# Layer 1 cluster attention of a four-layer decoder as one phase with unpadded heads, row tiles of 32, and key distances laid out with tokens on partitions

## The reference

```
def _affinity(t, centers, inv_two_sig2, amplitudes):
    t2 = jnp.sum(t * t, axis=-1, keepdims=True)
    c2 = jnp.sum(centers * centers, axis=-1)[None, :, None, :]
    tc = jnp.einsum('bhnd,hkd->bhnk', t, centers)
    d2 = jnp.maximum(t2 + c2 - 2.0 * tc, 0.0)
    return amplitudes[None, :, None, :] * jnp.exp(-d2 * inv_two_sig2[None, :, None, :])
q = split_heads(x @ W_q)
kk = split_heads(x @ W_k)
v = split_heads(x @ W_v)
...
q_aff = _affinity(q, centers, inv_two_sig2, amplitudes)
k_aff = _affinity(kk, centers, inv_two_sig2, amplitudes)
v_agg = jnp.einsum('bhnk,bhnd->bhkd', k_aff, v)
k_sum = jnp.sum(k_aff, axis=2)
num = jnp.einsum('bhnk,bhkd->bhnd', q_aff, v_agg)
den = jnp.einsum('bhnk,bhk->bhn', q_aff, k_sum) + EPS
out = num / den[..., None]
out = out.transpose(0, 2, 1, 3).reshape(b, n, dm)
return out @ W_o
```

## Time and profile before

| | us |
|---|---|
| median of 3 runs (4250.77 to 4256.24) | 4255.73 |
| the profiled execution | 4252.81 |
| its span, first to last instruction | 4251.0 |
| first DMA of the block to the start of its `centers` phase | 10.4 |
| `centers` | 6.0 |
| first normalisation, queries, keys and values | 26.9 |
| groups 0, 1, 2 | 93.6, 93.7, 93.7 |
| group 3 | 73.9 |
| the whole block | 398.2 |

### The profile page before, as it was taken

One profiled execution on the slowest core, in us unless ns is written; L12 is line 12 of the kernel. 1 busy time (PEld: TensorE's weight loads), 2 busy tenths in 40 slices (PEclk: granted clock), 3 DMA queues, 4 the chain that ended last, 5 costly groups with the idle time before them and its releaser, 6 DMA issues. The chain is left out here.

```text
span 4251.0 us, 54674 instructions
## 1 busy us (share of the span) xinstructions
PE 3446.1 (81%) x18236; PEld 2010.2 (47%) x18256; DVE 2230.5 (52%) x4573; ACT 1795.2 (42%) x4162; POOL 956.3 (22%) x1147
## 2 busy tenths in 40 slices
PE   6868559998588889963489989746799999998868
PEld 3535348876355545552245564534333333323535
DVE  5655534555333325537565535533688888864521
ACT  5847413332122214422255534301377777774311
POOL 2524434424200002210034442111111111111200
PEclk9978659999788879976689989858799999999979
DMA  9000326655100010000100000112200000000000
GB/s 308 22 17 1 131 91 208 210 170 152 60 0 0 0 41 1 1 30 0 47 1 1 1 1 21 51 67 70 82 16 16 16 16 23 16 1 22 1 22 20
DMA packets 153750, 207.56 MB, mean 49 GB/s; under 512 B 21699, under 2 KB 134212, under 8 KB 151652
## 3 DMA queue, kind: packets, MB, share of 16 engines
q1 hardware_dynamic: 139668, 166.50, 12.4%
q0 software_dynamic: 13824, 37.77, 2.7%
HBM read 115.98 MB, written 88.21 MB: 48 GB/s over the span
## 5 line engine op out<-in xcount | busy, mean ns | idle before, releaser
L3523 DVE TENSOR_REDUCE peaks<-ps 128x1 f32<-128x1024 f32 x512 | 608.6, 1220 | 147.9 <-PE ps L3469 142.7
L3551 ACT ACTIVATE attn<-ps 128x512 f32<-128x512 f32 x1024 | 535.4, 602 | 118.0 <-PE ps L3460 116.3
L3469 PE MATMUL ps<-keys,queries 96*128 96x512 bf16 x1024 | 396.3, 392 | 18.2 <-DMA keys<-parts 14.3
L3460 PE MATMUL ps<-queries,keys 99*128 99x512 bf16 x1024 | 389.9, 384 | 3.5 <-ACT attn L3551 2.7
L3482 PE MATMUL ps<-attn,head_values 128*32 128x512 f32 x2048 | 272.3, 604 | 0.0
L1040 POOL TENSOR_TENSOR attn_w<-attn_w,attn_share 128x512 f32<-128x512 f32 x128 | 133.0, 1044 | 514.9 <-DVE attn_share L928 514.9
L3460 PEld LDWEIGHTS ps<-queries,keys 99*128 99x128 bf16 x1024 | 99.0, 97 | 306.3 <-ACT attn L3551 222.0
L1729 PE MATMUL ps<-experts,tileT 128*128 x884 | 230.4, 383 | 4.3 <-issue 4.3
L1913 DVE COPY normed<-ps 128x256 f32<-128x256 f32 x221 | 93.7, 424 | 207.7 <-PE ps L1745 98.2
L1745 PE MATMUL ps<-experts,hiddenT 128*128 (+1 forms) x474 | 147.6, 394 | 28.1 <-DVE hiddenT L1922 25.1
L973 ACT ACTIVATE attn_w<-attn_w 128x512 f32<-128x512 f32 x128 | 80.2, 627 | 210.7 <-DVE attn_w L922 210.7
(11 more groups left out here) (600 smaller groups left out, 7390.0 us busy)
## 6 DMA issues: line engine op xcount, KB each, us to landing
tile_in<-routed_rows SPq DMA_DIRECT2D x244, 128.0 KB
expert_rows<-normed SPq DMA_DIRECT2D x221, 128.0 KB
routed_rows<-zeros SPq DMA_DIRECT2D x2, 8064.0 KB, 45.3
experts<-in_L_ffn_experts SPq DMA_DIRECT2D x4, 3072.0 KB
routed_rows<-zeros SPq DMA_DIRECT2D x1, 12160.0 KB, 62.6
experts<-in_L_ffn_experts SPq DMA_DIRECT2D x8, 1024.0 KB
parts<-parts SPq DMA_DIRECT2D x48, 128.0 KB, 1.8
queries<-parts SPq DMA_DIRECT2D x96, 64.0 KB, 2.2
```

The costliest lines, as they stand in the source:

```text
L3460: nc.tensor.matmul(bank(("score", n)), keys[h % 3][0:DEEP, sl(kt)], queries[h % 3][0:DEEP, sl(c, CHUNK)], start=True, stop=True).then_inc( ...
L3469: last = nc.tensor.matmul(k.ps[:, SB + p % PB, :], queries[h % 3][0:ROWS, sl(t)], keys[h % 3][0:ROWS, sl(c, CHUNK)], start=True, stop=True)
L3523: v.tensor_reduce(peaks[:, r % 2, i // 2, i % 2:i % 2 + 1], k.ps[:, at:at + 2, :], AX.XY, ALU.max).then_inc(s["maxed"], 1)
L3551: nc.scalar.activation(attn[:, n % RING, :], bank(("score", n)), ACT.Exp, scale=1.0 / 16.0).then_inc(s["read"], 1)
```

## The change

The phases from the first normalisation to the last addition become one phase, `affinity`, whose engines walk through slots g = -2 to 4. Heads are no longer padded: queries, keys and their squares are two tiles (T = 2) of 128 rows, eight heads each, and 32 rows hold a pair of heads. A **round** is one side, one tile, four pairs (R = 4): TensorE multiplies 32 rows at a time (`rows = sl(r, PAD)`), pair r into bank r of PSUM. For queries the table is stationary, as before. For keys the tokens are stationary and the table moves, so their affinities come out with tokens on partitions and the transposes go. Their scale is then no longer one number for a partition: it is multiplied into the tables beforehand, and the centers' squares times scale are added by a bf16 product of ones with three bf16 parts of them (`shift_parts`), four of 512 columns in a round. ScalarE takes the exponential straight from PSUM; the clip is a minimum with 1 afterwards, by VectorE in place. GpSimd makes all squares. The other work comes as **jobs** in the banks 4 to 7. The mix has the pooled values as the stationary operand (32 columns each), and the denominator is made in the same way from `sums`, so that the result is already turned; the division is over 512 tokens a tile.

```diff
+        def slot_work(g):
+            here, there = 0 <= g < GROUPS, 0 <= g + 1 < GROUPS
...
+            for i, kind in enumerate(("k", "k", "q", "q")):
+                if here:
+                    work.append(("round", kind, g, i % 2))
+                if i == 2 and 0 <= g - 1:
+                    work += [("project", g - 1, j) for j in range(GROUP)]
+                if there:
+                    work += [[("q", g + 1, 0)], [("q", g + 1, 1)], [("k", g + 1, 0)], [("k", g + 1, 1)]][i]
+            if here:
+                work += [("pool", g, j) for j in range(GROUP)]
+            if there:
+                work += [("v", g + 1, j) for j in range(GROUP)]
+            if 0 <= g + 2 < GROUPS:
+                work += [("x", g + 2, kt) for kt in range(KD)]
+            if here:
+                work += [(kind, g, t) for t in range(T) for kind in ("sum", "mix")]
+            return work
...
+                    if at:
+                        round_done(pe, "exped", ROUNDS[at - 1])
...
+                    if kind == "k":
+                        for r in range(R):
+                            every = shift_parts[:, R * t + r, :].unsqueeze(1).broadcast_to([P, GROUP, P])
+                            nc.tensor.matmul(k.ps[:, r, :], ones[:, :], every, start=True, stop=False)
+                    for part in range(2):
...
+                        if kind == "q":
+                            for r in range(R):
+                                rows = sl(r, PAD)
+                                last = nc.tensor.matmul(k.ps[:, r, :], table[rows, t, :], source[rows, t, :], start=part == 0, stop=part == 1)
+                        else:
+                            for j in range(GROUP):
+                                for r in range(R):
+                                    rows = sl(r, PAD)
+                                    last = nc.tensor.matmul(k.ps[:, r, sl(j)], source[rows, t, sl(j)], table[rows, t, :], start=False,
+                                                            stop=part == 1 and j == GROUP - 1)
...
-                        nc.vector.tensor_scalar(near[side][:, p, :], k.ps[:, m % 8, :], center2[:, p:p + 1], 0.0,
-                                                ALU.add, ALU.max).then_inc(s["bounded"], 1)
...
+                        v.tensor_scalar(tile, tile, 1.0, None, ALU.min).then_inc(s["capped"], 2)
...
+                    elif kind == "sum":
+                        last = v.tensor_scalar(share[:, i, :], source, 1e-6, None, ALU.add)
+                    else:
+                        link(v.reciprocal(share[:, i, :], share[:, i, :]))
+                        last = v.tensor_tensor(oT[:, i, :], source, share[:, i, :], ALU.mult)
...
+                for tile in (scales[:, :], key_scales[:, :, :]):
+                    link(v.tensor_scalar(tile, tile, 1e-3, None, ALU.max))
+                    link(v.tensor_tensor(tile, tile, tile, ALU.mult))
+                    link(v.reciprocal(tile, tile))
+                    link(v.tensor_scalar(tile, tile, -0.5, None, ALU.mult))
```

More of the change, by code:

```diff
@@ L2359, in l1_attn @@
     H, D, C = 16, 16, 64
-    PAIRS, T = H // 2, H * PAD // P
-    VW = D + 1
+    PAIRS, T, R = H // 2, 2, 4
+    VW, PW = D + 1, 2 * D
     n = "L1_attn_"
     with ExitStack() as stack:
-        wq, a = weights(k, stack, n + "W_q", KD, H * PAD)
-        wk, b = weights(k, stack, n + "W_k", KD, H * PAD)
+        wq, a = weights(k, stack, n + "W_q", KD, DIM)
+        wk, b = weights(k, stack, n + "W_k", KD, DIM)
         wv, c = weights(k, stack, n + "W_v", KD, DIM)
         wo, d = weights(k, stack, n + "W_o", KD, DIM)
[L2368 to L2383, removed]
@@ new lines, in l1_attn @@
+        centers, where = sb(k, stack, "centers", [P, T, P]), sb(k, stack, "where", [P, T, P])
+        key_centers, key_where = sb(k, stack, "key_centers", [P, T, P]), sb(k, stack, "key_where", [P, T, P])
+        scales, amplitude, shift = (sb(k, stack, m, [P, PAIRS]) for m in ("scales", "amplitude", "shift"))
+        key_scales = sb(k, stack, "key_scales", [P, PAIRS, P])
+        shift_parts, ones = sb(k, stack, "shift_parts", [P, PAIRS, P], BF16), sb(k, stack, "ones", [P, P], BF16)
+        xT = k.xT
@@ L2384, in _ @@
+        load_phase(k, loads)
+        with phase(k, "centers", "step exped squared summed cleared") as (block, s):
+            squares = near_q[:, 0, 0:T * P].rearrange("p (t c) -> p t c", t=T)
+            rest = near_k[:, 0:2, :].rearrange("p a (b c) -> p (a b) c", b=R)
             @block.vector
@@ new lines, in _ @@
+                v.tensor_scalar(centers[:, :, :], centers[:, :, :], -2.0, None, ALU.mult)
+                dve.wait_ge(s["summed"], 1)
+                link(v.tensor_tensor(shift[:, :].rearrange("p (t r) -> p r t", t=T), k.ps[:, 0:R, 0:T],
+                                     scales[:, :].rearrange("p (t r) -> p r t", t=T), ALU.mult))
+                for t in range(T):
+                    for r in range(R):
+                        rows = sl(r, PAD)
+                        v.tensor_tensor(key_centers[rows, t, :], centers[rows, t, :], key_scales[rows, R * t + r, :], ALU.mult)
+                        last = v.tensor_tensor(key_where[rows, t, :], where[rows, t, :], key_scales[rows, R * t + r, :], ALU.mult)
@@ L2533, in l1_attn @@
[L2533 to L2535 removed]
+                for t in range(T):
+                    for r in range(R):
+                        rows = sl(r, PAD)
+                        nc.tensor.matmul(k.ps[:, r, t:t + 1], squares[rows, t, :], k.ones[rows, 0:1], start=True, stop=True)
+                        last = nc.tensor.matmul(k.ps[:, R + r, sl(t)], k.ones[rows, :], squares[rows, t, :], start=True, stop=True)
```

327 lines of the change are left out of this document (209 added, 118 removed).

## The result

The changed kernel takes 4111.76 us, the median of 4 runs (4101.13 to 4116.81), against 4253.25 (4250.43 to 4256.24) of the kernel before on the same chip: a ratio of 0.9664, 95% interval 0.9643 to 0.9685. The forecast was 4101, range 4062 to 4170.

What follows compares the result with a forecast made beforehand. TensorE was taken to bound the block, much of its time going on zeros, small columns and half clock. Pipeline -175.9, `centers` +26.1 and loading -2 make -151.8 us from 4252.8: 4101 us, range 4062 to 4170.

Steps and rivals of the forecast that it cites:

- Row tiles: Key rounds: four row tiles of 32 run at once, 0.11 us per four, so 64 records take 1.8 us.
- The key round: Each slot's key rounds: ScalarE's four exponentials at 0.60, 2.5 us with gaps, hold the next round: 5.5 us a round.
- The query rounds: Two a slot, 16 records of 512 columns in 1.7 us each, with projection and key jobs: 10.3 us together.
- Setup: `centers` phase, nearly all VectorE's chain: 32.1 us against 6.0, ends 24 and 38; reciprocal of 1024 columns 6.55.
- Pool and values: In a slot: 64 pool records taken as 9 us, between 7.1 and 13.6; 16 values records as 5.5.
- The norm: Before x is turned, TensorE idles 4.6 us, as VectorE starts that norm only after the last values.
- The end: Slots 3 and 4: rounds 18.0, pool 9, first sum 1.3, two-reciprocal chain 10, projection 5, among others: 45.2 us.
- VectorE waited for elsewhere than at the norm: Sign of being wrong: in slots 0 to 2, VectorE is waited for at any place but the norm.
- another block moving by more than 3 us: Sign of being wrong: code outside the changed block, expected to stay at 3852.8 us, shifts by over 3 us.
- a low clock throughout: Rival: pipeline stays at the lower clock level, since holes keep it down; 24 us a slot, 4199 us; chance 0.12.
- tiles in pairs: Rival: keys' row tiles overlap only in pairs, +14 us, 4115 (one at a time 4143); chance for both 0.09.
- the other rival: Rival: the clock holds at 1.0 everywhere, pool 7.1, values 3.4, sums 3.5, so -22 us, 4079; chance 0.10.

Runs made afterwards that it cites:

- experiment 1: Changed kernel with the key round's two loops swapped, so records with the same 32 rows follow one another: block 288.9 us, ratio 0.9741.
- experiment 4: Changed kernel with the squares made by ScalarE from PSUM behind its copies instead of by GpSimd: block 251.3 us, ratio 0.9658.
- experiment 5: Changed kernel with a shorter `centers`: keys' scale by ScalarE's exponential, memsets on GpSimd, shift split on all rows at once: block 235.6 us, ratio 0.9614.
- experiment 3: Changed kernel with each pool piece followed by a values piece, instead of four pool then four values: block 240.6 us, ratio 0.9637.
- experiment 2: Changed kernel with VectorE taking the next rows' norm ahead of the pool's evictions: block 230.2 us, ratio 0.9604.
- experiment 7: Changed kernel with earlier norm, pool and values in turn, shorter setup, plus norm statistics between the key rounds' clips: block 206.5 us, ratio 0.9562.

## Why the prediction was right, and where it was off

| | forecast | measured |
|---|---|---|
| loading | 8.4 | 8.95 |
| `centers` | 32.1 | 32.24 |
| slots -2, -1 | 25.4 | 24.73 |
| slot 0 | 45.5 | 45.72 |
| slot 1 | 47.9 | 51.01 |
| slot 2 | 41.9 | 41.39 |
| slots 3, 4 | 45.2 | 50.11 |
| block | 246.4 | 254.15 |

- **Row tiles**, the step on which most hung, held: fours every 0.125 us (0.11 forecast, from four column tiles), and experiment 1 prices the other case at 34.7 us.
- **The key round** takes 5.2 us, not 5.5. Its four exponentials last 0.60 each but start 0.49 apart, 2.07 in all; I had taken 0.6 and gaps, 2.5. The query rounds more than make up for it: their exponentials, with a scale and a bias, last 0.78 and start 0.67 apart (four in 2.79), and the two query rounds of slot 1 with their jobs took 11.7 us against 10.3.
- **Setup.** The reciprocal of 1024 columns took 6.55 us, what the earlier trace rows gave by a straight line. The one-row steps cost what 128 rows do, as taken.

```profile
1150.21 6.55 DVE L2406 RECIPROCAL key_scales<-key_scales 128x1024 f32<-128x1024 f32 x1
...
1166.67 0.68 DVE L2428 COPY key_scales<-near_k 1x1024 f32<-1x1024 f32 x1
```

- The Trainium skill ("VectorE: DVE Perf Modes", the fixed hardware budget) had given 8.3 ns a column by my estimate; the row shows 6.4 with the fixed part, and the measurement decides.
- **Pool and values**: 9 + 5.5 = 14.5 forecast, 14.1, 17.4 and 15.6 in slots 0 to 2. In this profile slot 1 is the place most off, but in experiments 1, 4 and 5 the same stretch took 15.7, 14.1 and 15.6, so the term was some 0.6 us a slot too small (15.1 on average) and the rest of slot 1's excess belongs to this execution. The mechanism (a row of 34-column records lowers the clock) is shown by experiment 3; how far into the row it falls differs between slots and executions, and no run says why.
- **The norm** stood in the way by 4.5 us (4.6 forecast). That the hole also lowers the clock of what follows stood chiefly in the sums (6 "after the idle time", against 3.5; they took 4.9 and 5.1). Taking the norm out of the way was worth 21 to 24 us and not 13.4 (experiment 2).
- **The end** lasted 50.1 instead of 45.2: the rounds of slot 3, with no jobs under the key rounds, 19.6 (18.0), the first sum at half clock 2.0 (1.3), the chain of the reciprocals 10.7 (10), the projection wholly at half clock 6.7 (5).
- **Luck**: slots 0 to 2 came out well in part because errors cancelled. In slot 0 the rounds took 20.3 us (19.0 forecast) and the sums 4.9 (6).
- **Squares by GpSimd at no cost**: held, by experiment 4.
- **VectorE waited for elsewhere than at the norm**, one of my signs of being wrong, happened twice: TensorE waited 0.39 us for the additions of the projection (L2641) in slots 1 and 2. It is too little to change the reading.
- The remaining 8 us between 4101 and the profiled 4116.8 are the block's later start, less 2.5 behind it. I had written that another block moving by more than 3 us would speak against the reading; it moved by 10, but by the starts of the other executions (up to 1130.5) that is for the most part the spread of what lies ahead, not the change. What causes that spread was not tried.
- **The rivals**: a low clock throughout would have shown 0.5 in the slots, they show 0.76 to 0.88; tiles in pairs would have shown 64 records in 3.6 us. The full clock of the other rival came only with the edits of experiment 7.

## What to carry to other kernels

When heads are narrower than the array, lay 32 rows to a head pair and walk the row tiles in the innermost loop; here that was most of the gain, and the order of two loops was worth 35 us. In a pipeline of one phase, look for every spot where TensorE waits or runs only narrow products, since behind the long ones the granted clock fell and the cost came out well above the hole (21 to 24 us for 13.4 us of norm holes, 10 us for two waits of 1.2); fill them with wide products that were due anyway. Before putting work of VectorE ahead of its evictions, count how long the free PSUM banks will feed TensorE in the new order.

## What the runs showed of the hardware

- The granted clock over 80 records of pool and values was 0.61 to 0.76 with the narrow ones on end and 1.00 with narrow and wide in turn, TensorE busy throughout in both (experiment 3).
- Exponentials of 128x512 from PSUM start every 0.49 us with plain input (each lasts 0.60) and every 0.67 with scale and bias by partition (each lasts 0.78).
- Some of VectorE's steps slow beside GpSimd's memsets, in the shorter setup: the first step below, of 8 columns, takes 0.17 in the changed kernel, where GpSimd has no memset in this phase, and a step of the same kind with 1024 columns took 1.17 beside the memsets and 0.69 behind them.

```profile
1078.41 0.95 POOL L2433 MEMSET pooled<- 128x1024 f32 x1
1078.53 0.87 DVE L2401 TENSOR_SCALAR scales<-scales 128x8 f32<-128x8 f32 x1
1079.31 0.97 POOL L2434 MEMSET sums<- 128x1024 f32 x1
1079.43 0.17 DVE L2402 TENSOR_TENSOR scales<-scales 128x8 f32<-128x8 f32 x1
```

The Trainium skill ("GPSIMD Engine Reference", Specifications) says that the two engines share their SBUF interfaces and contend where a VectorE instruction runs in a mode with two ports or reads two inputs from SBUF. The rows agree in part: the first step, with one input, ends with the first memset, but the last one reads two inputs under the second memset and is not slowed. No row tells in which mode a step ran. GpSimd's squares beside the pipeline cost nothing that experiment 4 could see.
